# A layernorm, scan and FP4 feed-forward kernel: halves of the sequence in turn, normalisation on ScalarE, y parts added on GpSimd, and new orders

## What is computed

```python
def _L0_attn_ref(x, ...):
    phazor = jnp.exp((phazor_angle * 1j - decay) * ln_phazor_scale)
    filt = (phazor[None, :] ** t) * phazor_init[None, :]
    conv = jnp.fft.ifft(fft(filt) * fft(x), axis=1)[:, :length]
    y = (conv + last_conv * phazor ** (t + 1)) * (1.0 - jnp.exp(-decay * ln_phazor_scale))
    return y.real
def fp4_quant_dequant(x):          # blocks of 16 along the last dimension
    scale = jnp.maximum(jnp.max(jnp.abs(xb), axis=-1, keepdims=True) / 6.0, 1e-12)
    xn = xb / scale
    return _GRID[jnp.searchsorted(_MID, jnp.abs(xn))] * jnp.sign(xn) * scale
def fp4_linear(x, w):
    return jnp.einsum('bsk,nk->bsn', fp4_quant_dequant(x), fp4_quant_dequant(w))
...
xn = _layernorm(x, axis=-1)                                  # x is (4, 1024, 128)
h = jax.nn.silu(fp4_linear(xn, w_gate)) * fp4_linear(xn, w_up)   # 352 columns
out = x + _L0_attn_ref(xn, ...) + fp4_linear(h, w_down)
```

## Time and profile before

| | us |
|---|---|
| median of 3 runs (132.09 to 132.13) | 132.12 |
| span of the profiled execution, first to last instruction | 131.0 |
| outside the span | 1.1 |

### The profile page before, as it was taken

How to read it: one execution, slowest core, us unless ns; L and a number is a source line. 1 busy time by engine, 2 the same in 40 slices (tenths; PEclk the granted TensorE clock), 3 DMA queues, 4 the chain that set the end, 5 groups by cost and what they waited for, 6 DMA issues and landing times. The chain is left out here.

```text
span 131.0 us, 2333 instructions
## 1 busy us (share of the span) xinstructions
PE 114.4 (87%) x657; PEld 86.2 (66%) x657; DVE 106.0 (81%) x217; ACT 100.8 (77%) x198; POOL 102.4 (78%) x145
## 2 busy tenths in 40 slices
PE   3800799999949999999999999999799999999992
PEld 3700355446528777757777887777586888788792
DVE  0867949898699879999879998987699899998610
ACT  4287563998858699997799979876959797939840
POOL 4698998699999989999999998994978499630000
PEclk9985555999995999999999999999999999999999
DMA  3990000000000000002001100200020020020202
GB/s 120 323 343 31 3 0 3 0 3 0 0 0 5 0 0 0 0 9 76 0 0 43 39 5 3 80 0 0 0 80 5 0 80 0 0 85 0 83 0 80
DMA packets 3323, 4.90 MB, mean 37 GB/s; under 512 B 496, under 2 KB 1392, under 8 KB 3312
## 3 DMA queue, kind: packets, MB, share of 16 engines
q1 hardware_dynamic: 3168, 4.77, 10.6%
q10 hardware_dynamic: 144, 0.00, 0.1%
HBM read 2.67 MB, written 2.10 MB: 36 GB/s over the span
## 5 line engine op out<-in xcount | busy, mean ns | idle before, releaser
L1140 PE MATMUL ps_u<-wu_T,xq_T 128*128 128x352 f32 x64 | 24.5, 492 | 2.6 <-DVE hq L1590 2.6
L1125 PE MATMUL ps_g<-wg_T,xq_T 128*128 128x352 f32 x64 | 26.0, 489 | 0.1
L1191 PEld LDWEIGHTS ps_o<-wd_T,hq_T 128*128 128x128 f32 x174 | 23.1, 200 | 2.5 <-issue 0.7
L1191 PE MATMUL ps_o<-wd_T,hq_T 128*128 128x128 f32 x174 | 24.4, 285 | 0.0
L807 ACT COPY hq_T<-ps_h 128x384 f32<-128x384 f32 x32 | 15.2, 474 | 6.9 <-PE ps_h L1159 6.8
L801 ACT ACTIVATE silu<-ps_g 128x352 f32<-128x352 f32 x32 | 14.8, 463 | 3.3 <-PE ps_g L1125 2.9
L1590 DVE TENSOR_TENSOR hq<-ps_u,den 128x704 f32<-128x704 f32 (+1 forms) x17 | 14.2, 833 | 2.7 <-PE ps_u L1147 2.7
L1159 PE MATMUL ps_h<-ident,hq 128*128 128x128 f32 x96 | 16.2, 279 | 0.1
L1140 PEld LDWEIGHTS ps_u<-wu_T,xq_T 128*128 128x128 f32 x64 | 11.4, 200 | 7.1 <-DVE hq L1590 3.1
L1159 PEld LDWEIGHTS ps_h<-ident,hq 128*128 128x128 f32 x96 | 12.1, 145 | 5.1 <-issue 3.4
L1545 DVE TENSOR_TENSOR ps_u<-silu,ps_u 128x704 f32<-128x704 f32 (+1 forms) x17 | 14.3, 841 | 1.4 <-PE ps_u L1140 0.8
(11 more groups left out here) (166 smaller groups left out, 248.8 us busy)
## 6 DMA issues: line engine op xcount, KB each, us to landing
x_all<-x_in SPq DMA_DIRECT2D x8, 256.0 KB, 5.1
out<-x_all SPq DMA_DIRECT2D x7, 256.0 KB, 2.0
w_raw<-w_in SPq DMA_DIRECT2D x2, 192.0 KB, 3.9
out<-x_all SPq DMA_DIRECT2D x4, 64.0 KB, 1.6
w_raw<-w_in SPq DMA_DIRECT2D x1, 176.0 KB, 3.9
par<-params_in ACTq DMA_DIRECT2D x1, 3.5 KB, 3.0
```

The costliest lines, as they stand in the source:

```text
L1125: pe.matmul(ps_g[:, 0:I], x_cols(t), wg_T[:, :], start=True, stop=True).then_inc(s_gate, 1)
L1140: pe.matmul(slot(q)[:, j, 0:I], x_cols(t), wu_T[:, :], start=True, stop=True).then_inc(s_up, 1)
L1191: m = pe.matmul(out_cols(t), hq_T[t % NHT][:, c * P:(c + 1) * P], wd_T[:, c, :], start=False, stop=(c == NCH - 1), skip_group_check=True)
```

## The change

Group g is now half g // 4 of batch g % 4: the first halves of all batches come first, then the second halves. All states at the ends of the first halves stand in one tensor, so the state is turned once for four batches: two small instructions on ScalarE (turn_part) and two on VectorE (turn_state). u and y of a group have their real and imaginary part in one tensor, and one GpSimd instruction makes both. For groups 1 to 6 (Y_POOL) GpSimd then adds the two parts of y (add_y_parts), and sum_parts has one matmul a tile instead of two. For pairs 11 and 13 (H_POOL) ScalarE copies the rounded codes out of PSUM (copy_codes) and GpSimd scales them (scale_codes), in place of scale_h on VectorE.

All normalisation is on ScalarE (XN_POOL is empty). turn_xn writes its transposes into ps_x with the step of four, and copy_xnT is a plain copy. The large constants are immediate values instead of columns of a tensor. The first two tiles are divided into the output bank by VectorE (divide_first), rounded there by TensorE (round_first) and scaled by VectorE (scale_first); the halved inverse deviation of group 0 is no more in its scales but in the silu and in the product of its four tiles. centre moves from GpSimd to VectorE. The first weights are loaded ahead of the second x tiles. TensorE opens its banks first, has 24 warm-up transposes behind that, and three times four more between the first roundings. The orders of all engines are new.

```diff
+    Y_POOL = [1,2,3,4,5,6]
+    H_POOL = [11, 13]
...
-    x_tiles = x_in.rearrange("b (h p j) d -> (b h) p j d", j=TG, p=P)
-    out_tiles = out.rearrange("b (h p j) d -> (b h) p j d", j=TG, p=P)
+    WARM = 24
+
+    x_tiles = x_in.rearrange("b (h p j) d -> h b p j d", j=TG, p=P)
+    out_tiles = out.rearrange("b (h p j) d -> h b p j d", j=TG, p=P)
...
+            load_x(0)
+            load_w(0)
+            load_x(1)
+            load_w(1)
+            load_w(2)
...
-            def centre(j):
-                pool.wait_ge(s_tot, 1)
-                pool.tensor_scalar(xc[:, j * D:(j + 1) * D], x_all[:, j, :], 2.0, total[:, j:j + 1],
-                                   ALU.mult, ALU.subtract).then_inc(s_xc, 1)
...
+                pool.tensor_tensor(u[g % NU][:, :, :], in_tab[:, :, :],
+                                   xn_T[g % NU][:, :].unsqueeze(1).to_broadcast([P, 2, GT]), ALU.mult).then_inc(s_u, 1)
...
+                pool.tensor_tensor(y[g % NY][:, :, :], state[:, g % B, :, :], out_tab[:, :, :],
+                                   ALU.mult).then_inc(s_y, 1)
+
+            def add_y_parts(g):
+                pool.wait_ge(s_y, g + 1)
+                pool.tensor_tensor(y[g % NY][:, 0, :], y[g % NY][:, 0, :], y[g % NY][:, 1, :],
+                                   ALU.add).then_inc(s_ysum, 1)
+
+            def scale_codes(q):
+                pool.wait_ge(s_code, H_POOL.index(q) + 1)
+                if q >= NH:
+                    pool.wait_ge(s_hT, PAIR * (q - NH + 1))
+                pool.tensor_tensor(hq_blocks(q), code_blocks(q), pair_scales(den[q % ND], 0, PAIR),
+                                   ALU.mult).then_inc(s_hqp, 1)
...
+            def turn_part(k):
+                act.wait_ge(s_gim, B)
+                act.wait_ge(s_init, 7)
+                act.mul(turn_parts[:, k, :], last_state(1),
                         (neg_turn, cos_t[:, GT:GT + 1])[k]).then_inc(s_part, 1)
 
-            def turn_state(b, k):
-                re = g_re[2 * b % NST][:, GT - 1:GT]
-                act.wait_ge(s_gre, 2 * b + 1)
-                act.wait_ge(s_part, 2 * b + k + 1)
-                act.activation(turned[:, b, k:k + 1], re, ACT.Identity, scale=(cos_t, sin_t)[k][:, GT:GT + 1],
-                               bias=turned[:, b, 2 + k:3 + k]).then_inc(s_turned, 1)
+            def half_rstd():
+                act.wait_ge(s_stat[0], STAT_STEPS)
+                act.mul(half_rs[:, :], rstd[:, 0:TG], 0.5).then_inc(s_half, 1)
...
+                act.wait_ge(s_ln, stat_of(g) + 1)
+                act.activation(xn[g][:, j * D:(j + 1) * D], x_all[:, t, :], ACT.Identity,
+                               scale=rstd[:, t:t + 1], bias=shift[:, t:t + 1]).then_inc(s_xna, 1)
...
-                act.copy(in_tiles(xn_T[g % NU]), ps_x[:, :].rearrange("d (j p) -> d j p", j=TG)).then_inc(s_xnTc, 1)
+                    act.wait_ge(s_u, g - NU + 1)
+                act.copy(xn_T[g % NU][:, :], ps_x[:, :]).then_inc(s_xnTc, 1)
...
+                if t < TG:
+                    act.wait_ge(s_half, 1)
+                    act.activation(silu[q % NS][:, j, :], ps_g[:, 0:I], ACT.Silu,
+                                   scale=half_rs[:, t:t + 1]).then_inc(s_silu, 1)
+                else:
+                    act.activation(silu[q % NS][:, j, :], ps_g[:, 0:I], ACT.Silu).then_inc(s_silu, 1)
...
-                act.activation(big[n % NB][:, j0:j1, :], sqh[n % 2][:, j0:j1, :], ACT.Identity,
-                               bias=base_c).then_inc(s_big, 1)
+                act.activation(big[n % NB][:, j0:j1, :], sqh[n % 2][:, j0:j1, :], ACT.Copy,
+                               bias=BASE).then_inc(s_big, 1)
+
+            def copy_codes(q):
+                k = H_POOL.index(q)
+                act.wait_ge(s_hr, q + 1)
+                if k >= NC:
+                    act.wait_ge(s_hqp, k - NC + 1)
+                act.copy(code_of(q)[:, :, :], in_slot(q)).then_inc(s_code, 1)
...
-                for _n in range(16):
-                    pe.transpose(ps_o[:, 0:P], ident[:, :], ident[:, :])
+                for _n in range(WARM):
+                    pe.transpose(ps_g[:, 0:P], ident[:, :], ident[:, :])
+
+            def open_banks():
...
+            def open_first():
+                pe.wait_ge(s_unit, 1)
+                for c in range(2):
+                    m = pe.matmul(ps_o[:, c * P:(c + 1) * P], unit[0][:, :], unit[0][:, :],
+                                  start=(c == 0), stop=(c == 1))
+                m.then_inc(s_fopen, 1)
+
+            def keep_warm(_n):
+                for _k in range(4):
+                    pe.transpose(ps_g[:, 0:P], ident[:, :], ident[:, :])
+
+            def round_first():
+                pe.wait_ge(s_fbig, 1)
+                pe.wait_ge(s_unit, 2)
+                pe.matmul(first_half(ps_o), unit[0][:, :], first_half(xbig[0]), start=False, stop=False,
+                          skip_group_check=True)
+                pe.matmul(first_half(ps_o), unit[1][:, :], first_half(xbig[0]), start=False, stop=True,
+                          skip_group_check=True).then_inc(s_fr, 1)
...
-                    m = pe.transpose(ps_x[:, j * P:(j + 1) * P], xn[g][:, j * D:(j + 1) * D], ident[:, :])
+                    m = pe.transpose(in_tiles(ps_x[:, :])[:, j, :], xn[g][:, j * D:(j + 1) * D], ident[:, :])
...
-                pe.wait_ge(s_yre, g + 1)
-                pe.wait_ge(s_yim, g + 1)
+                if g in Y_POOL:
+                    pe.wait_ge(s_ysum, Y_POOL.index(g) + 1)
+                else:
+                    pe.wait_ge(s_y, g + 1)
...
-                pe.matmul(out_cols(t), in_tiles(y_re[g % NY])[:, j, :], ident[:, :], start=False, stop=False,
-                          is_transpose=True, skip_group_check=True)
-                pe.matmul(out_cols(t), in_tiles(y_im[g % NY])[:, j, :], ident[:, :], start=False, stop=True,
-                          is_transpose=True, skip_group_check=True).then_inc(s_sum, 1)
+                parts = 1 if g in Y_POOL else 2
+                for k in range(parts):
+                    m = pe.matmul(out_cols(t), in_tiles(y[g % NY][:, k, :])[:, j, :], ident[:, :], start=False,
+                                  stop=(k == parts - 1), is_transpose=True, skip_group_check=True)
+                m.then_inc(s_sum, 1)
...
+                if PAIR * q < TG:
+                    dve.wait_ge(s_half, 1)
+                    for j in range(j0, j1):
+                        t = PAIR * q + j
+                        dve.wait_ge(s_silu, t + 1)
+                        dve.wait_ge(s_up, t + 1)
+                        dve.scalar_tensor_tensor(in_slot(q, j, j + 1), in_slot(q, j, j + 1), half_rs[:, t:t + 1],
+                                                 silu[q % NS][:, j:j + 1, :], ALU.mult, ALU.mult).then_inc(s_h, 1)
+                    return
...
+            def turn_state(k):
+                dve.wait_ge(s_part, k + 1)
+                dve.wait_ge(s_gre, B)
+                dve.scalar_tensor_tensor(turned[:, k, :], last_state(0), (cos_t, sin_t)[k][:, GT:GT + 1],
+                                         turn_parts[:, k, :], ALU.mult, ALU.add).then_inc(s_turned, 1)
...
+            def divide_first():
+                dve.wait_ge(s_xrec, 1)
+                dve.wait_ge(s_fopen, 1)
+                dve.tensor_tensor(blocks(first_half(ps_o)), blocks(first_half(xc)),
+                                  spread(first_inv), ALU.mult).then_inc(s_fv, 1)
+
+            def scale_first():
+                dve.wait_ge(s_fr, 1)
+                dve.tensor_tensor(blocks(first_half(xv[0])), blocks(first_half(ps_o)),
+                                  spread(den_x[0][:, xblks(0, 0)]), ALU.mult).then_inc(s_fq, 1)
```

985 lines of the change are left out of this document (486 added, 499 removed).

## The result

The changed kernel takes **126.27 us** (median of 4 runs, 126.16 to 126.37) against 132.12 before: ratio 0.953, 95% interval 0.949 to 0.957. Run again beside later experiments (e14) it gave 0.956 (0.949 to 0.963). The forecast was 129.5 with a range of 127.0 to 133.0. Medians and ratios of the experiments leave out executions more than 1.5% above the fastest of the same kernel (one of e4, one of e7, four of e7b), but the profile of e7b is of such a one.

The account below looks back on a forecast made before the run. ScalarE's in-order chain was taken to bound the start up to round_h(2), TensorE's own work everything behind: 42.8 + 78.1 + 5.2 gaps + 2.3 to the span's end + 1.1 to the median = 129.5 us, range 127.0 to 133.0.

Parts of the forecast that it names:

- the cut: Start of round_h(2), the rounding of the third pair of tiles, where time is divided: 44.27 us before, 42.8 forecast.
- In-order waits come on top ... I take 1.8: ScalarE ahead of round_h(2): 1.8 us of waits put big_h(2)'s end at 42.7; the bound without waits was 41.
- ledger of 31.9: ScalarE's summed work from the second unit matrix, about 9.0, to the end of big_h(2): 31.9 us, against 25.3 before.
- + 5.2 gaps: TensorE behind round_h(2)'s start: 5.2 us of gaps and small waits, taken over from the kernel before.
- Rival 1: Start goes better and gaps shrink: no in-order waits (-1.8), the tail wins 0.9; 126.9 us, chance 0.10.
- turn_state ... so nothing: turn_state on VectorE waits once for all batches, product(9) queued behind; inputs a scan older, so cost nothing.
- about equal, 72 of 84 us, hidden: VectorE loses two scale_h, gains centring, two splits and the first tile's division and scaling: load about equal, hidden.
- ScalarE behind the cut "-1.4": ScalarE's work from round_h(2) on, with 15 normalisations taken over, changes by about -1.4 us; not the bound there.
- rival 4: GpSimd's y additions come late and TensorE idles for what it saved and a little less: 131.9 us, chance 0.08.
- rival 3: turn_xn's strided PSUM write costs TensorE in full, +2.7 to 3.1 us: 132.4, half of it 131.0; chance 0.14.
- rival 5: A table switch costs twice its load, 3 x 1.28 us more on ScalarE ahead of round_h(2): 133.3, chance 0.02.
- +1.1 to the median: Time added between the end of the profiled span, 131.0 us before, and the median of 132.12: 1.1 us.

Follow-up runs that it names:

- e14: The changed kernel itself run once more, unchanged, beside later experiments: ratio 0.956 to the kernel before.
- e4: The changed kernel with two more 128x512 copies on ScalarE, about 1.05 us, ahead of the first silu, read by nobody: 128.75 us, ratio 0.973 to before.
- e7: The changed kernel with the sixteen normalisations of groups 4 to 7 moved back from ScalarE to GpSimd: 136.5 us, ratio 1.026 to before.
- e7b: The changed kernel with the sixteen normalisations of groups 4 to 7 back on GpSimd, but queued earlier there than in e7: ratio 0.997 to before.
- e2: The changed kernel with Exp as ScalarE's first function and the cosine straight behind sine and fold, two table loads less behind the second unit matrix: 125.04 us, ratio 0.944.
- e6: The changed kernel without the 24 warm-up transposes and the three times four that keep TensorE busy in between: ratio 0.954 to before.
- e8: The changed kernel with VectorE scaling pairs 11 and 13 itself again, without ScalarE's code copies and GpSimd's scale_codes: 129.02 us, ratio 0.976.
- e1: The changed kernel with turn_part's products first copied by VectorE from SBUF into PSUM, where turn_state reads them: 125.02 us, ratio 0.946 to before.
- e12: The changed kernel with turn_state's first operand four adjacent identity-matrix elements in SBUF instead of the last states, so no long step: 126.54 us, run once.
- e5: The changed kernel with turn_xn writing side by side into PSUM and the step of four words back in ScalarE's copy_xnT: 128.45 us, ratio 0.967.
- e3: The changed kernel without GpSimd's six additions, TensorE adding both y parts again in all groups: 129.09 us, ratio 0.976 to before.
- e9: The kernel before with GpSimd adding the two y parts of groups 1 to 6, 24 fewer matmuls on TensorE: 138.03 us, ratio 1.040.
- e13: The kernel before with turn_xn writing with a step of four words and ScalarE's copy_xnT contiguous: ratio 1.002 to before.

## Why the prediction was wrong

- **The view was right**: TensorE's own work behind the cut, ScalarE's order ahead of it (e2, e4). The 78.1 us of plain work stand (78.0 measured).
- **First failing step, "In-order waits come on top ... I take 1.8" on a ledger of 31.9.** ScalarE waited for 0.9 us and worked for 31.0: both terms were too large by 0.9, and together they gave the bound of 41 that the step had named for "no wait". That is -1.9 us; that the cut fell on that bound is luck. Which term of the ledger is too high was not taken apart, nor which of the moved instructions keeps ScalarE fed. That the warm-up does not, e6 shows.
- **Second failing step, "+ 5.2 gaps", carried over unchanged.** They were not a constant of the kernel: 5.1 became 3.0, of which 1.8 are new. Of the 5.1, 2.2 lie at four waits with a releaser: 0.9 at 92.41 behind GpSimd's normalisation, 0.5 at 122.78 for the refill in the tail, and 0.4 each at two more. The other 2.9 are pieces of 0.3 us or less. Of the 3.0 left, 1.8 are the stall behind turn_state, 0.4 a wait for copy_hT in the tail and 0.8 small pieces. The lines of three of the waits before (the fourth stands above, at 92.41):

```profile
61.26 0.66 PE L1110 MATMUL ps_x<-ident,xv 128*128 128x128 f32 x4 [0.23 <-POOL xv L464]
...
68.57 0.62 PE L1147 MATMUL ps_u<-big,unit 128*128 128x352 bf16 x3 [0.24 <-ACT big L822]
...
122.78 0.36 PE L1179 MATMUL ps_o<-ident,y_re 128*128 128x128 f32 x1 [0.32 <-ACT ps_o L832]
```

The change took two kinds of work off the engines that TensorE waits for, and undoing either brings excess back: the scaling of two pairs on VectorE makes 5.6 (e8), sixteen normalisations on GpSimd 9.7 or 12.8 (e7b, e7). The prediction priced both only as load ("It gets lighter", "hidden"), not by who waits in order for them. How the 2.9 us of small pieces divide among these and the new orders is open. Rival 1 said that gaps may shrink, but gave it 0.9 us in the tail and a chance of 0.10; its terms make 126.8, near the measured time, without the stall of turn_state and with a wrong base.
- **"turn_state ... so nothing" was wrong**, by +1.5 us (e1), for the reason that e12 shows. Without it the miss would have been larger. Its wait on all batches cost nothing that the list shows; its operands did.
- **"about equal, 72 of 84 us, hidden" for VectorE** came out right in the sum (73.35 us), but the codes moved to GpSimd were worth 2.3% (e8): not hidden at all, because VectorE is at 0.92 to 0.99 between 95 and 115 us, which the mean over 84 us doesn't show.
- **ScalarE behind the cut "-1.4"** went right in direction (69.88 to 68.17). It has no free room there all the same: 3.6 us more of copies cost 1.0 (e5).
- **Right**: ScalarE under 3 us idle ahead of the cut (0.9), TensorE over 97% busy behind it, the additions' price (2.8, e3), no late addition (rival 4), the strided write at nothing (rival 3), the loads of 1.28 with nothing behind them (rival 5), 0.39 us for a normalisation in a row, the tail (0.4 won of at most 0.9). None of the prediction's signs of being wrong came, though its time was wrong: they looked only at the slower side.
- **"+1.1 to the median" was a slip of the base**, not an effect of the change: outside the span lie 2.0 us now and 2.1 before. The cut at 44.27 belongs to a profiled execution about 1.0 us longer than the median, the 132.12 to others. With 2.1 in its place the sum would have been 130.5, and 42.8 a gain of 0.5 us at the start over the 43.3 of a median execution, not 1.5. What lies outside the span the profile doesn't show.

Together: -1.9 (start) -2.1 (from the cut on: excess -2.2, plain work -0.1, rounding) +0.9 (outside) is -3.2 us within rounding, 129.5 to 126.3. The +0.9 hid part of the miss.

## To carry to other kernels

Gaps on the bounding engine are not a term to carry over: list each with its releaser, follow it one queue further back, and ask of each whether the change removes or lengthens it. A part of a change can be worth nothing or cost 4% alone and pay with the others (e9 against e3, e13 against e5), because in-order queues set what comes late. A small VectorE step with both tensor operands in SBUF can last as long as the GpSimd instruction beside it; here one operand in PSUM freed it. And before a time is taken apart by a profile, see that the profiled execution is of the same kind as the median: its span and its mean granted clock, beside those of the other runs, tell.

## What the runs showed of the hardware

- VectorE steps of 128x4 with two SBUF operands took 0.90 to 1.20 us beside GpSimd, 0.22 with one in PSUM, with the same step of 4 KB.
- TensorE wrote transposes into PSUM with a step of four words at 273 ns against 272; the same step cost ScalarE 1110 against 590 ns.
- The row of granted clocks showed full speed while a gate tile took 1.44 us (e6), as long as in a stretch granted 0.50 (1.43) and not as at 1.00 (0.78): the duration of a known matmul is a second reading of the clock.
- The half clock at the start lay at other times in two profiles of the same kernel (16.8 to 20.2 us, 11.4 to 14.8 us); the third rounding was 0.3 us apart.
- A second stretch at half clock (0.71 in 40 to 45 us) came in some executions of the kernel before and not in others, behind gaps of 1.9 to 2.2 us in all three profiles, and went with about 1.0 us: spans of 130.7 to 131.5 against 129.9 to 130.3.
